# A routed expert block on one core: the first product of every pair formed transposed, with the expert's weight blocks stationary and the transposed tokens moving

## The reference, cut to what matters

```python
expert_ids = jnp.minimum(tid // tokens_per_expert, E - 1)        # 4 experts, by token id
for e in range(E):                                               # Wg = Wu = Wd = ctx_2048
    g = jax.nn.silu(jnp.einsum('bsd,fd->bsf', hidden_states, Wg[e]))
    u = jnp.einsum('bsd,fd->bsf', hidden_states, Wu[e])
    y = jnp.einsum('bsf,df->bsd', g * u, Wd[e])
    out = jnp.where((expert_ids == e)[..., None], y, out)
...
h = jax.nn.relu(jnp.einsum('btd,edr->betr', x, Wd) + bd[None, :, None, :])
eo = jnp.einsum('betr,erd->betd', h, Wu) + bu[None, :, None, :]
out = jnp.einsum('bte,betd->btd', w, eo)                         # w: softmax gates of the top 2 of 8
...
x = x + jnp.tanh(g_xattn[0]) * _L0_xattn_ref(_layernorm(x, axis=-1), itok, ctx, ctx, ctx)
x = x + jnp.tanh(g_ffn[0]) * _L0_ffn_ref(_layernorm(x, axis=-1), Wr, br, Wd, bd, Wu, bu)
```

## Time and profile before

| | |
|---|---|
| time, median of 3 runs | 203.06 us (202.65 to 203.64) |
| the profiled execution | span 201.4 us from the first to the last instruction; no other time of it is given, so 1.7 us of the median lie outside the span or between executions |
| TensorE matmul (PE) | 175.0 us busy, 87% of the span, 1074 matmuls |
| TensorE weight load (PEld) | 104.0 us busy, 52%, beside the matmuls |
| VectorE (DVE) | 155.7 us, 77% |
| ScalarE (ACT) | 111.9 us, 56% |
| GpSimd (POOL) | 99.7 us, 50% |
| mean granted TensorE clock | 0.974 of full speed |

### The profile page before, as it was taken

How to read it: one execution, slowest core, us unless ns; L and a number is a source line. 1 busy time by engine, 2 the same in 40 slices (tenths; PEclk the granted TensorE clock), 3 DMA queues, 4 the chain that set the end, 5 groups by cost and what they waited for, 6 DMA issues and landing times.

```text
span 201.4 us, 4382 instructions
## 1 busy us (share of the span) xinstructions
PE 175.0 (87%) x1074; PEld 104.0 (52%) x1075; DVE 155.7 (77%) x523; ACT 111.9 (56%) x224; POOL 99.7 (50%) x246
## 2 busy tenths in 40 slices
PE   1576896999997989999999999999999999976560
PEld 1564463655553656656656556655665655534310
DVE  4859696697768799889888998797877878678640
ACT  2596599884287166473665726547265561545200
POOL 4478846427246366375553735516244162445641
PEclk9999999999999999999999999999999999999955
DMA  5947572101210201203101011011010100101121
GB/s 135 370 163 231 205 216 69 52 5 20 86 55 0 52 0 52 59 0 104 55 0 54 0 52 52 2 52 52 0 54 0 52 20 33 52 0 55 52 104 52
DMA packets 6784, 13.43 MB, mean 67 GB/s; under 512 B 2392, under 2 KB 2520, under 8 KB 6768
## 3 DMA queue, kind: packets, MB, share of 16 engines
q0 software_dynamic: 2560, 8.39, 12.6%
q1 hardware_dynamic: 4208, 4.86, 7.3%
HBM read 9.06 MB, written 4.19 MB: 66 GB/s over the span
## 4 chain that ended last, share of the span: by engine, by line
PE 44%; issue 18%; POOL 10%; DVE 9%; DMA 7%; ACT 4%; DVEq 3%; SPq 2%; POOLq 1%; ACTq 0%
PE ps_y L603 6%; PE ps_y L605 6%; PE ps_y L604 6%; PE ps_a L603 4%; PE ps_a L605 4%; PE ps_a L604 4%; DMA xs<-in_x_dram,rows_of 4%; ACT h L796 3%; POOL rs L457 3%; PE ps_h2T L685 2%; PE ps_pT L624 2%; DMA bu_nat<-in_L_ffn_bu_dram 2%; POOL hot_slot L432 2%; PE ps_hT L677 2%; POOL xs L439 2%
## 5 line engine op out<-in xcount | busy, mean ns | idle before, releaser
L456 POOL TENSOR_SCALAR ve<-mv 128x1 f32<-128x1 f32 x32 | 7.7, 239 | 62.6 <-DVE mv L1099 51.8
L796 ACT ACTIVATE h<-xs,mrs,rs 128x512 f32<-128x512 f32 (+1 forms) x16 | 21.1, 1317 | 22.4 <-POOL mrs L458 22.4
L783 ACT ACTIVATE pT_hi<-ps_pT 128x512 f16<-128x512 f32 x19 | 11.3, 595 | 36.0 <-PE ps_pT L624 36.0
L603 PE MATMUL ps_y<-w_hi,pT_hi 128*128 x76 | 28.8, 379 | 2.3 <-DVE w_lo L952 1.5
L603 PE MATMUL ps_a<-w_hi,hT_hi 128*128 x76 | 29.1, 382 | 0.7 <-DVE hT_lo L1074 0.6
L604 PE MATMUL ps_a<-w_lo,hT_hi 128*128 x76 | 29.1, 382 | 0.0
L605 PE MATMUL ps_a<-w_hi,hT_lo 128*128 x76 | 29.0, 381 | 0.0
L604 PE MATMUL ps_y<-w_lo,pT_hi 128*128 x76 | 28.8, 379 | 0.0
L605 PE MATMUL ps_y<-w_hi,pT_lo 128*128 x76 | 28.8, 379 | 0.0
L1086 DVE SCALAR_TENSOR_TENSOR xs<-ps_y,y_t,xs 128x512 f32 x19 | 14.3, 750 | 10.2 <-PE ps_y L605 7.7
L529 POOL DMA_INDIRECT out_dram<-xs,rows_of x16 | 17.3, 1083 | 5.9 <-DVE xs L1117 3.5
(11 more groups left out here) (209 smaller groups left out, 424.0 us busy)
## 6 DMA issues: line engine op xcount, KB each, us to landing
w_nat<-in_ctx_dram SPq DMA_DIRECT2D x4, 1024.0 KB, 7.9
xs<-in_x_dram,rows_of POOLq DMA_INDIRECT x16, 3.6
wd_nat<-in_L_ffn_Wd_dram SPq DMA_DIRECT2D x1, 256.0 KB
wu_nat<-in_L_ffn_Wu_dram SPq DMA_DIRECT2D x1, 256.0 KB
out_dram<-xs,rows_of POOLq DMA_INDIRECT x16, 2.9
b_in<-in_L_ffn_bd_dram SPq DMA_DIRECT2D x1, 64.0 KB
bu_nat<-in_L_ffn_bu_dram SPq DMA_DIRECT2D x3, 16.0 KB
tok_i<-in_itok_BxS_dram SPq DMA_DIRECT2D x1, 8.0 KB, 1.8
```

Of the source, the lines that this page charges most:

```text
L603: mm(ps[:, :], lhs_hi[:, kc, :], hi, start=(kc == 0), stop=False)
L796: a(h2[:, :, :], x1[:, col(k), :].rearrange("p o (q c) -> p c (o q)", c=KC), ACT.Identity, bias=mrs[:, 1, col(k)], scale=rs[:, 1, col(k)]) ...
```

## The change

The first product is formed the other way round. A block of 128x128 of the expert's weights is stationary and the 128 tokens of the pair are the moving columns, so that the output is `a` transposed: the 128 partitions of `ps_a` are the features of a block, and its columns are four blocks of 128 tokens. silu and the product work element by element and stay as they are. `prod` is then transposed already: `transpose_product`, its semaphore and its reads from PSUM go, and the split into `pT_hi` and `pT_lo` reads `prod` in SBUF, seen through the view `prodT`.

```diff
+        prodT = prod[:, :].rearrange("p (c q) -> p c q", c=KC)
...
-        pT_done = sem("pT_done")
...
+            def split_product_T(ps, rhs_hi, rhs_lo, e):
+
+                for m in range(KC):
+                    cols = slice(m * P, (m + 1) * P)
+                    for kc in range(KC):
+                        hi = w_hi[:, bass.ds(e, 1), kc, cols].rearrange("p e n -> p (e n)")
+                        lo = w_lo[:, bass.ds(e, 1), kc, cols].rearrange("p e n -> p (e n)")
+                        mm(ps[:, cols], hi, rhs_hi[:, kc, :], start=(kc == 0), stop=False)
+                        mm(ps[:, cols], hi, rhs_lo[:, kc, :], start=False, stop=False)
+                        last = mm(ps[:, cols], lo, rhs_hi[:, kc, :], start=False, stop=(kc == KC - 1))
+                return last
...
-            def transpose_product(k):
-
-                pe.wait_ge(prod_done, k + 1)
-                for c in range(KC):
-                    last = tr(ps_pT[:, c, :], prod[:, c * P:(c + 1) * P], ident[:, :])
-                last.then_inc(pT_done, 1)
...
-                if has_y and not has_a:
-                    transpose_product(i - 1)
                 if some(T, -3 - LATE, i0) and (has_y or some(NP, -2, i0)):
                     hidden_product(i - 3 - LATE)
-                if has_y and has_a:
-                    transpose_product(i - 1)
...
                     pe.wait_ge(hT_lo_done, k + 1)
-                    split_product(ps_a, hT_hi, hT_lo, e_now).then_inc(a_done, 1)
+                    split_product_T(ps_a, hT_hi, hT_lo, e_now).then_inc(a_done, 1)
...
-                    act.wait_ge(pT_done, k + 1)
+                    act.wait_ge(prod_done, k + 1)
                     wait_last(act, y_done, k)
-                    a(pT_hi[:, :, :], ps_pT[:, :, :], ACT.Copy).then_inc(pT_hi_done, 1)
+                    a(pT_hi[:, :, :], prodT, ACT.Copy).then_inc(pT_hi_done, 1)
...
-                v.tensor_tensor(pT_lo[:, :, :], ps_pT[:, :, :], pT_hi[:, :, :],
+                v.tensor_tensor(pT_lo[:, :, :], prodT, pT_hi[:, :, :],
                                 ALU.subtract).then_inc(pT_lo_done, 1)
```

## The result

The changed kernel takes **207.94 us** (median of 4 runs, 207.35 to 208.48) where the kernel before takes 203.22 (4 runs): ratio 1.0233, interval [1.0203, 1.0263]. The forecast had the direction and the mechanism of the larger part of the loss, and its range held the time; its size was 2.4 us, and 4.7 were measured. In the experiments, executions over 1.5% above the fastest of the same kernel are left out of the medians and ratios (three of ten of e1, one of ten of f1, one of four of h1, two of ten of h2); the traces of f1 and h2 are of such executions.

A forecast was written before the change was run, and what follows sets the result against it. TensorE was taken to bound the kernel, a second chain about as long, with its sequencer pacing the new product. Start 1.95, steps 0.75 and tail -0.3 gave +2.4 on 203.06: 205.4 us, range 202.0 to 208.6.

The forecast's parts named there:

- What bounds the kernel: TensorE is busy throughout full steps of 8.29 to 8.4 us, with a second chain through VectorE, GpSimd and ScalarE about as long.
- The array's side: In the first product, 48 matmuls of 128 columns take 2.7 to 2.8 us against 2.59 before.
- The rival by which loads bind at 81 ns: Weight loads set the first product's pace, 3.9 us: +14, 217 us; chance 0.07 together with a clock fall.
- the rival on code: The longer loop body is fetched again in each of five passes, 2.5 us each: +12, 215 us; chance 0.05.
- The sequencer's side: TensorE's sequencer needs 0.24 us for each of 16 groups, so the first product takes 3.85 us unless it starts well ahead.
- Pairs 0 and 1 at nothing: At the start, first products longer by 0.8 to 1.2 us go into TensorE's existing waits: 0.
- Pair 2, +0.55; pair 3, +1.15; pair 4, +0.25; pairs 5 and 6 hidden: Ahead of the full steps, longer first products delay the second block's stream by about 1.95 us; later losses meet waits for h2.
- The loop: In the eleven full steps, steps without the branch stay at 8.3 us; five passes with it lose 0.75 us in all.
- The tail: Behind the last pair the transposes go, but VectorE had waited only 0.30 us for pT_hi: -0.3 us.
- pT_hi and pT_lo read SBUF instead of PSUM: In the split of prod, each instruction changes by at most 0.1 us either way, free but for a few tenths over the kernel.
- no change: Losses of pairs 2 to 4 go into waits for h2, the second chain holds the steps: +0.9 at most, 203.5 us; chance 0.20.
- Faster: The array sets the first product's pace and TensorE gains 0.33 us a pair where it bounds: 2.6 us, 200.5 us; chance 0.12.

The follow-up runs named there:

- e1: The changed kernel with the first product on expert 0's weights at fixed addresses for every pair (output wrong); 203.37 us, ratio 1.0003.
- f1: The changed kernel with each group's third matmul reading the high weights again, so one register instruction a group; 203.99 us, ratio 1.0028.
- h1: The kernel before with pT_lo subtracting from prod in SBUF, so both its inputs lie in SBUF; 205.98 us, ratio 1.0138.
- h2: The changed kernel with prod in PSUM and expert 0's fixed addresses in the first products of pairs 0 to 7; 203.41 us, ratio 0.9993.
- g1: The changed kernel with prod written to PSUM in place of SBUF; 206.85 us, ratio 1.0201.
- g2: The changed kernel with prod in PSUM and expert 0's fixed addresses in every first product; 202.14 us, ratio 0.9939.
- f4: The changed kernel with the removed transposes' semaphore still allocated, unused; 206.99 us in one run.
- e3: The kernel before with the first product's 512 columns cut in four, 48 matmuls of 128, transposes kept; 207.66 us, ratio 1.0224.
- e4: The changed kernel with a pair's expert register kept for its second product instead of loaded again; 209.44 us.
- g3: The changed kernel with expert 0's fixed addresses in the first products of pairs 0 to 7 only; 206.03 us, ratio 1.0142.

## Why the forecast was right in kind and half in size

The whole, by medians: the sequencer's pace costs 4.7 us (g1 206.85 against g2 202.14), the missing transposes give 1.1 back (g2 against 203.21 of before), the held GpSimd takes 1.1 (207.94 against g1). That these add up to the 4.7 measured is no check, since each is the difference of neighbours in one row of four kernels. The last is also the least sure, since the intervals of the changed kernel and of g1 overlap; by the starts of the y products, f4 against g1, it is 1.0, of which f4's drain, with its later fall of the clock, gives 0.8 back. Point by point:

- **What bounds the kernel**: right. TensorE's steps were full, and each delay of the product ahead of the loop was paid.
- **The array's side**, 2.7 to 2.8 us: right, 2.68 with fixed addresses at 0.056 us a matmul. The rival by which loads bind at 81 ns has nothing for it; the code queue moved 10 packets instead of 6 and the eleven steps show no gap of the 2.5 us a pass that the rival on code had priced.
- **The sequencer's side**, 0.24 us a group: right, 0.247 at pair 3, and shown as the cause by e1, e3 and f1.
- **Pairs 0 and 1 at nothing**: right. In f4 the first y product starts 0.03 us later than before.
- **Pair 2, +0.55; pair 3, +1.15; pair 4, +0.25; pairs 5 and 6 hidden**: measured where nothing else disturbs (g1 less before, by the second, third, fourth and fifth y product, each less what it had at the one before) 0.84, 1.29, 0.26 and 0: 2.4 against 1.95. Two of these terms were also worked out loosely. For pair 2 the forecast's own numbers, 42.85 less 42.38, give 0.47 and not 0.55; and the 42.38 is read from the chain, which puts that row 0.16 later than the order of time does (42.22). For pair 3 they give 3.85 - 2.6 = 1.25.
- **The loop**: 0.9 in the eleven steps, against 0.75: right. The first product takes about 2.8 and 3.4 us in turn in the middle of the loop, where the leads of 0.9 and 0.5 us gave 2.95 and 3.35. That the leads hang on the loads of the experts was wrong, by e4. The step ahead of the eleven was left out of the sum: +0.35 at the seventh y product.
- **The tail**, -0.3: right, -0.4 from the 18th to the last y product.
- These terms make 3.2 in g1's trace where the forecast had 2.4; by medians g1 is 3.6 above before. This is the mis-sized part: pairs 2 and 3 and the seventh step.
- **"pT_hi and pT_lo read SBUF instead of PSUM ... 0.1 either way for each is my bound"**: the step that failed. On their own engines it holds (628 ns for 0.60; 690 for 0.69). I looked only at the reader's duration and not at who else reads SBUF while VectorE does. The price lay on GpSimd, whose chain I had named in the same section as the one that holds the steps: about 1 us, a fifth of the loss, where the forecast had nothing.

Of the two rivals that were near, "no change" assumed that the losses of pairs 2 to 4 would go into waits for h2; they did not, since those waits come behind y products that the losses had already moved. "Faster" is what g2 shows once both costs are gone, at 0.6% and not the 2.6 us that were priced: in most steps the second chain holds.

A form of the new product that needs one register instruction a group with all its matmuls was not run, and no version of the change with the right output beats the kernel before. Of the kernels whose output is whole, f3, the kernel before with the bias moved, is the fastest.

## What to carry to other kernels

Count the addresses that come from registers, not the matmuls: cutting one matmul into four with an address each leaves the array's time alone and multiplies the sequencer's, and the cut binds as soon as a group's register instructions take longer than its matmuls. When a tile moves from PSUM to SBUF, ask of each VectorE instruction that reads it whether both inputs now lie in SBUF, and what GpSimd does at that time. And look twice at a changed kernel before a wait in its trace is put down to the change: a second trace took 1.1 us off the list here.

## What was not expected of the hardware

- A GpSimd instruction of one column was held for 0.6 us, until VectorE's two-input instruction had ended, although its own operands are other tiles (0.88 against 0.29 us; all eight traces with both inputs in SBUF show it, and none of the nine with one in PSUM).
- TensorE's clock fell to 1.2 GHz in one y product behind an idle of the array of 2.35 us (g3, f1), 2.2 (h2) and 2.0 (h1), and up to the last y product it stayed at 2.4 behind 1.9 (g2) or less in all traces; e1's trace had 2.3 and no fall. So the idle alone does not decide it. Where it fell it cost about 1.7 us, in h1 three times the 0.6 by which the idle had grown.
- Two register instructions of 46 and 32 ns by their rows take 0.11 us and more each of the sequencer's pace; their rows alone would have made the pair 0.08.
